# Attention and expert kernel: the second normalisation's tiles move from VectorE to ScalarE

## What is computed

```python
# attention stage, per batch
sim = (ctx @ Wq.T per head) . (ctx @ Wk.T per head) / (sqrt(32) * 4)      # 512 x 512
thr = 153rd largest of each row of sim
A = sigmoid(sim) * (sim >= thr)
A = (A + A.T) * 0.5
g = sigmoid(gamma_raw)
x = x + (1 - g) * layernorm(x) + g * A
# feed-forward stage
h = layernorm(x)                      # the normalisation that is changed
x = x + shared_expert(h) + top-2 of 8 experts of h, weighted by the router's softmax
```

## Time and profile before

| | us |
|---|---|
| median of 3 runs | 544.81 |
| the three runs | 543.98, 544.81, 548.53 |
| the profiled execution, its own time | 547.91 |
| its span, first to last instruction | 546.2 |

### The profile page before, as it was taken

The page is one execution under the profiler, slowest core; times in us unless marked ns, Lnnn a source line. Parts: engine busy times, 40 slices in busy tenths (PEclk is TensorE's granted clock), DMA queues, the critical chain, the costliest instruction groups (busy, mean ns, idle before and its releaser), DMA issues.

```text
span 546.2 us, 9363 instructions
## 1 busy us (share of the span) xinstructions
PE 460.9 (84%) x2826; PEld 260.9 (48%) x2827; DVE 342.8 (63%) x900; ACT 233.3 (43%) x410; POOL 186.3 (34%) x233
## 2 busy tenths in 40 slices
PE   5202598999999998989989699998999999999970
PEld 2001344445444544444555466665666666666630
DVE  3898999999999999817983545555445422222210
ACT  5562467158815881352424344434344422222210
POOL 2100320035002500250775144444445454545431
PEclk9755769999999999998999899999999999999985
DMA  8700540027202700273137757787778555445441
GB/s 278 214 1 1 177 151 2 1 92 196 42 1 86 141 6 2 78 155 107 42 96 193 255 137 184 178 190 158 189 176 198 89 94 95 77 77 87 89 77 19
DMA packets 36941, 60.48 MB, mean 111 GB/s; under 512 B 6169, under 2 KB 16665, under 8 KB 36898
## 3 DMA queue, kind: packets, MB, share of 16 engines
q0 software_dynamic: 10384, 23.34, 23.9%
q1 hardware_dynamic: 26514, 36.60, 21.2%
HBM read 37.64 MB, written 22.28 MB: 110 GB/s over the span
## 4 chain that ended last, share of the span: by engine, by line
DVE 39%; PE 35%; DMA 11%; issue 6%; POOL 4%; ACT 2%; SPq 0%; DVEq 0%; POOLq 0%; ACTq 0%
DMA out_dram<-xb,sidx 6%; DVE stats L1139 5%; PE bank L1060 3%; PE bank L1062 3%; PE bank L1061 3%; PE bank L1036 3%; PE bank L1037 3%; PE bank L1038 3%; PE bank L1040 3%; PE bank L1041 3%; PE bank L1039 3%; DVE below L1180 3%; DVE sgt L1360 2%; DVE hS L1349 2%; PE bank L1022 2%
## 5 line engine op out<-in xcount | busy, mean ns | idle before, releaser
L901 PE MATMUL bank<-xT,W 128*128 128x512 f16 x176 | 68.5, 389 | 1.9 <-DVE sgt L1360 1.9
L902 PE MATMUL bank<-xT,W 128*128 128x512 f16 x176 | 68.5, 389 | 0.0
L903 PE MATMUL bank<-xT,W 128*128 128x512 f16 x176 | 68.3, 388 | 0.0
L539 POOL DMA_INDIRECT out_dram<-xb,sidx x35 | 56.7, 1620 | 29.7 <-POOL sidx L538 28.7
L1472 DVE TENSOR_TENSOR hS<-bank,hS 128x384 f16<-128x384 f32 x35 | 19.5, 557 | 73.8 <-ACT hS L783 73.8
L1467 DVE SCALAR_TENSOR_TENSOR xb<-bank,sgt 128x352 f32<-128x352 f32 x35 | 18.3, 524 | 58.0 <-ACT sgt L777 58.0
L777 ACT ACTIVATE sgt<-bank 128x352 f32<-128x352 f32 x35 | 16.2, 463 | 90.0 <-PE bank L1041 90.0
L791 ACT ACTIVATE xb<-bank,wcol 128x512 f32<-128x512 f32 x35 | 24.1, 687 | 56.3 <-PE bank L1062 56.3
L480 POOL TENSOR_TENSOR rstd<-pw 128x4 f32<-128x4 f32 x12 | 16.1, 1344 | 87.9 <-DVE pw L1148 87.8
L1036 PE MATMUL bank<-W,xT 128*128 x140 | 44.2, 315 | 0.5 <-issue 0.5
L1037 PE MATMUL bank<-W,xT 128*128 x140 | 44.1, 315 | 0.0
(11 more groups left out here) (235 smaller groups left out, 1071.5 us busy)
## 6 DMA issues: line engine op xcount, KB each, us to landing
xn_dram<-W SPq DMA_DIRECT2D x16, 256.0 KB, 2.0
out_dram<-W POOLq DMA_DIRECT2D x12, 256.0 KB, 5.5
stage<-L_ffn_down_w_in SPq DMA_DIRECT2D x12, 256.0 KB, 2.8
sim<-L_ffn_down_w_in SPq DMA_DIRECT2D x12, 256.0 KB, 3.0
stage<-L_ffn_gate_w_in SPq DMA_DIRECT2D x16, 176.0 KB, 2.6
stage<-L_ffn_up_w_in SPq DMA_DIRECT2D x16, 176.0 KB, 2.8
sim<-L_ffn_gate_w_in SPq DMA_DIRECT2D x16, 176.0 KB, 3.0
sim<-L_ffn_up_w_in SPq DMA_DIRECT2D x16, 176.0 KB, 3.6
```

What stands on the lines that cost most here:

```text
L539: pool.indirect_dma_start(out=out, out_offset=bass.IndirectOffsetOnAxis(ap=sidx[:, p:p + 1], axis=0), in_=y2[:, p, :], in_offset=None, com ...
L901: pe.matmul(o, wh, xT[:, 0, c, :], start=(c == 0), stop=False)
L902: pe.matmul(o, wh, xT[:, 1, c, :], start=False, stop=False)
L903: last = pe.matmul(o, wl, xT[:, 0, c, :], start=False, stop=(c == KD - 1))
```

## The change

ScalarE gets a `normalise(b, t)` of its own that rewrites a tile in place with an Identity activation, factor and addend per partition from a new small buffer `nrm`. It runs tiles 0 and 1 ahead of the first half precision copy, and tile t + 2 behind copy t. VectorE keeps the two small operations, which now write `nrm`, and goes on to the next batch. The wait for the residual's store moves to ScalarE.

```diff
+    nrm = sb("nrm", [P, 2, TB])
...
+    s_nrm = sem("s_nrm")
...
+        def normalise(b, t):
+            g = TB * b + t
+            if t == 0:
+                act.wait_ge(s_nrm, b + 1)
+                act.wait_ge(d_x1, 16 * TB * (b + 1))
+            act.activation(xs[b % 2][:, t, :], xs[b % 2][:, t, :], ACT.Identity, bias=nrm[:, 1, t:t + 1],
+                           scale=nrm[:, 0, t:t + 1]).then_inc(s_xn, 1)
+
...
             if b + 1 < NB:
                 for t in range(TB):
                     scores(b + 1, t)
+            normalise(b, 0)
+            normalise(b, 1)
             for t in range(TB):
                 xn_hi(b, t)
+                if t + 2 < TB:
+                    normalise(b, t + 2)
...
             dve.wait_ge(s_rstd, 3 * b + 3)
-            link(dve.tensor_scalar(rstd[:, :], rstd[:, :], XS, None, ALU.mult))
-            link(dve.scalar_tensor_tensor(aff[:, 1, :], mv[:, :, 0], -1.0, rstd[:, :], ALU.mult, ALU.mult))
-            dve.wait_ge(d_x1, 16 * TB * (b + 1))
-            for t in range(TB):
-                dve.tensor_scalar(xs[b % 2][:, t, :], xs[b % 2][:, t, :], rstd[:, t:t + 1], aff[:, 1, t:t + 1], ALU.mult,
-                                  ALU.add).then_inc(s_xn, 1)
+            if b:
+                dve.wait_ge(s_xn, TB * b)
+            link(dve.tensor_scalar(nrm[:, 0, :], rstd[:, :], XS, None, ALU.mult))
+            dve.scalar_tensor_tensor(nrm[:, 1, :], mv[:, :, 0], -1.0, nrm[:, 0, :], ALU.mult, ALU.mult).then_inc(s_nrm, 1)
+            dve.wait_ge(s_nrm, b + 1)
```

## The result

| | median us | runs |
|---|---|---|
| before | 545.76 | 17 |
| changed | 549.64 | 17 |

The ratio is 1.0068 (1.0038 to 1.0098): some 3.7 us more, where 2.6 were forecast and 547.4 us as the time. The same kernel timed twice more gave 1.0006 (0.9979 to 1.0033) and 1.0112 (1.0069 to 1.0155). The profiled execution of the changed kernel took 551.62 us, its span is 549.8.

A forecast was written before the change was run, and what follows sets the result against it. VectorE was taken to carry the attention stage, its freed time lost waiting for GpSimd's power. 0.9 + 0.3 + 0.3 + 1.1 = + 2.6 us takes the median from 544.81 to 547.4 us, range 543.5 to 550.6 us.

The forecast's parts named there:

- The step that carried it: Batches 0 to 2: VectorE's saved 2.76 us each go into waiting for GpSimd's power, queued behind subtractions fed by ScalarE.
- Batch 0: Power behind all four subtractions starts at 70.5, VectorE goes on at 71.55 after waiting; + 0.9 us.
- Batch 1: Power behind three subtractions, VectorE's first use still blocked 1.11 us by the fourth; + 0.3 us.
- Batch 2: Same as batch 1: power behind three subtractions, first use blocked by the fourth; + 0.3 us.
- Batch 3: Tile, copy, subtraction, transposes, output copies, store: the last output copy moves later; + 1.1 us.
- I costed TensorE's clock at nothing: Behind batch 3: TensorE carries the rest with no work added or removed, so it was costed at nothing.
- Busy times: Whole kernel, sign of being right: VectorE's falls by some 10 us, ScalarE's rises by some 13, span hardly moved.
- VectorE's time coming off: Rival: batches 0 to 2 each save 2.76 us, batch 3 loses 1.1; 537.6 us, chance 0.06.
- A draw by the race at the fourth subtraction: Rival: batches 1 and 2, race goes the other way or power starts earlier; 545.2 us, chance 0.14.
- ScalarE serialising on its own waits: Rival: waits on ScalarE's own tiles break the overlap of normalise and copy; 550.6 us, chance 0.12.
- the lower bound: ScalarE's tiles and copies: overlap holds throughout, 1.23 us a tile, against 1.43 if nothing overlaps.
- the forecast's sign of being wrong: Behind batch 3: TensorE's part changes its own length, which the sum leaves out.

The follow-up runs named there:

- the held kernel: Kernel before, with GpSimd's fourth subtraction in batches 1 and 2 held until nprobe is written; 0.9958, then 0.9987.
- the kernel without tiles: Kernel before with the four normalising instructions left out in every batch, nothing in their place; rounds of 53.69 and 53.67 us.
- the held version of the change: Changed kernel, batch 3 on VectorE, power ahead of all subtractions, these held until nprobe, ScalarE's first count ahead of transposed-tile copies; 0.9985.
- the power second: Changed kernel with GpSimd's power for the next threshold directly behind the first subtraction in batches 0 to 2; 1.0014.

## Why the prediction was right, and where it was off

**The step that carried it** was not to book VectorE's 2.76 us as a gain, because the next thing VectorE needs comes through ScalarE's copies and GpSimd's queue. All of it is in the rows: the power at 70.99 (70.5 forecast), the idle times of 3.36 and 2.23 us (one to two and a half forecast), the 1.11 us of blocking unchanged in batches 1 and 2.

**The terms.** Batch 0: + 0.9 forecast, + 0.70 measured with the clock up (56.22 against 55.52), + 1.4 with it low. Batch 1: + 0.3 forecast, + 0.33 measured. Batch 2: + 0.3 forecast, + 0.55 measured; 0.31 of it is nprobe's, and 0.24 comes later, where VectorE idles for 0.24 us in batch 3's threshold, by the code for GpSimd's all-reduce; it is there in every kernel with changed batches 0 to 2 and not with batch 3 changed alone, and I have no cause for it. Batch 3: + 1.1 forecast, + 1.06 measured with the clock up, + 2.4 with it low. Sum: 2.6 forecast, 2.6 measured with the clock up, and 4.6 to 4.7 with it low. That the sum comes out to the tenth is in part luck: batch 0 was put 0.2 us too high and batch 2 0.25 too low.

**What was missed** is one term: I costed TensorE's clock at nothing, and in two of three executions it made some 2.0 us, 0.6 to 0.7 in batch 0 and 1.4 in batch 3. In batch 0 the changed kernel is more exposed to it. There the fourth score copy started at 61.73 before and at 63.72 in the changed kernel's first execution, though all that runs before 63.5 is the same code. That by itself is chance: the held kernel has it at 63.63 in its first execution and 61.68 in its second, and its round 0 hardly cares (55.63 and 55.55), since VectorE's own tiles cover the time until ScalarE is free. In the changed kernel the first tile is ScalarE's, behind the score copies; it starts at 64.22 in place of 63.55, and the round is 0.7 us longer. The cover was removed with the work. The forecast took the copies of the earlier trace rows into the sum for batches 1 and 2, but not for batch 0, where they had ended early in the execution that I read. In batch 3 it is not shown that the low clock belongs to the change: of the six traces with ScalarE normalising there, two have it at the nine products, and of the eight others none.

**Busy times.** VectorE was to fall by some 10 us and fell by 8.2: the tiles made 11.0 us, but its pw operation of each next batch is blocked by a subtraction now (1.05 us in batch 0, 0.85 in batches 1 and 2, 2.0 more in all), which the forecast doesn't have. ScalarE was to rise by 13 and rose by 9.9, since tiles and copies overlap and are counted once.

**The rivals.** VectorE's time coming off: out, by the wait for the power, and by the kernel without tiles it could not have been 2.76 us anyway. A draw by the race at the fourth subtraction: GpSimd won it in all three traces of the changed kernel. ScalarE serialising on its own waits: out, a pair of tiles takes 1.51 us, a tile starts 0.52 us behind a copy and the next copy 0.70 behind that tile, so the lower bound was right. The limit that I didn't name is TensorE's, 0.6 us short of VectorE's: it doesn't touch the forecast, but it kills the gain in the held version of the change.

**The whole time.** The median is 2.2 us above the forecast: 0.95 of it since more executions put the kernel before at 545.76 and not at 544.81, the rest since the two medians lie 3.9 us apart and not 2.6. 307 us lie behind the last store in the profile before, 306 in the first execution of the changed kernel and 303 in the second, with no code changed there; so the forecast's sign of being wrong, a TensorE part of another length, came up and can't be told from scatter. That scatter is larger than the 2.6 us, and it goes with the clock: of the twelve executions of the second run, one of 545.8 us had a mean granted clock of 0.938, one of 550.19 us had 0.926. The three ratios go the same way. In the run that gave 1.0112 the changed kernel's clocks lay at 0.918 to 0.927 and those of the kernel before at 0.919 to 0.938; in the run that gave 1.0006 they lay at 0.923 to 0.941 and 0.922 to 0.939. That this is all of the difference is not shown, since each run has one trace. Only the attention part of the traces, the same to 0.01 us in batches 1 and 2, bears the explanation.

## What to carry to other kernels

Before booking the time of work that is taken off the busiest engine, look up what that engine asks for next and who makes it: if the maker sits behind the same work in an in-order queue, the time turns into a wait. Then look for the second bound; here it stood 0.6 us short of a chain that seemed to carry everything. And work on the busy engine can be the cover for another engine's late arrival, so moving it can make the kernel more sensitive to that, as in batch 0 here (a low clock costs its round 0.7 us in place of 0.1).

## What the runs showed of the hardware

VectorE operations on four numbers a partition, begun while GpSimd runs a subtraction of 128 x 512 with both inputs in SBUF, end when that subtraction does: they take 1.05 to 1.12 us when it has just begun, 0.44 (69.09, kernel before) and 0.37 us (66.47, second execution of the changed kernel) late in it, and 0.15 to 0.17 us otherwise. That holds for operations with two tensor inputs and for pw with one. The statistics of full tiles (two in 1.27 us, beside a subtraction and without one) were not held up by it. Holding one subtraction back by a semaphore for 0.86 us makes a round 0.9 us shorter.

TensorE's granted clock differs between executions of the same program at the same places (0.51 and 1.00 over the same nine products), with the same idle times ahead of them. In all three executions of the changed kernel the two low stretches came together or not at all, but they are not tied: with batch 3 alone changed and with the power second, the clock was 0.51 and 0.54 from 57 to 63 us and 1.00 over the nine products.
